# A two-layer graph attention kernel: chunk 0 and chunk 1 of the adjacency turned by column quarters, first score rows loaded from ScalarE

## The reference, cut to what matters

```
Wh = (h @ W).reshape(N, H, D)                      # layer 0: H = 4 heads, D = 32
e = leaky(s_src[:, None] + s_dst[None, :])         # 4096 x 4096 for each head
e = where(adj > 0, e, NEG_INF); attention = softmax(e, axis=1)
x = layernorm(x + elu(attention @ Wh))
...                                                # layer 1: one head over all 128 features
x = layernorm(x + proj(expmap0(attention1 @ logmap0(x))))
```

## Time and profile before

| what | value |
|---|---|
| median of 3 runs | 948.96 us (948.72 to 950.5) |
| profiled execution, its own time | 949.88 us |
| span of the profile | 946.1 us |
| TensorE busy | 840.5 us, 89% of the span |
| VectorE busy | 789.7 us, 83% |
| ScalarE busy | 660.4 us, 70% |
| GpSimd busy | 19.1 us, 2% |
| mean granted TensorE clock | 0.952 |

### The profile page before, as it was taken

One profiled execution on the slowest core, in us unless ns is written; L12 is line 12 of the kernel. 1 busy time (PEld: TensorE's weight loads), 2 busy tenths in 40 slices (PEclk: granted clock), 3 DMA queues, 4 the chain that ended last, 5 costly groups with the idle time before them and its releaser, 6 DMA issues.

```text
span 946.1 us, 23426 instructions
## 1 busy us (share of the span) xinstructions
PE 840.5 (89%) x10348; PEld 686.9 (73%) x10348; DVE 789.7 (83%) x1433; ACT 660.4 (70%) x846; POOL 19.1 (2%) x39
## 2 busy tenths in 40 slices
PE   6089699999899987999699979779999999999993
PEld 6089689988899987999699876435555555555551
DVE  4699499999988999999689998789495977777876
ACT  2598698999769998799698894876454463647112
POOL 1000000000000000000000000000000000000000
PEclk9589799999899999999799989889999999999997
DMA  8999999996577002301000505240704040321000
GB/s 151 160 184 128 193 109 140 190 125 65 113 129 97 25 2 69 69 14 14 1 14 25 124 2 112 77 101 1 208 16 90 12 89 18 84 65 37 12 18 7
DMA packets 151344, 73.06 MB, mean 77 GB/s; under 512 B 138182, under 2 KB 142792, under 8 KB 150984
## 3 DMA queue, kind: packets, MB, share of 16 engines
q1 hardware_dynamic: 146484, 54.68, 26.1%
q0 software_dynamic: 4608, 16.78, 17.2%
q10 hardware_dynamic: 148, 0.07, 0.0%
HBM read 83.96 MB, written 21.12 MB: 111 GB/s over the span
## 4 chain that ended last, share of the span: by engine, by line
PE 49%; DVE 26%; ACT 10%; SPq 5%; DMA 5%; issue 4%; POOL 0%; DVEq 0%; ACTq 0%; POOLq 0%
PE bank L552 30%; PE bank L542 19%; ACT ring L595 7%; SPq L320 5%; DVE ring L792 5%; DVE ring L805 4%; DMA adj_small<-in_adj_dram 3%; ACT below L644 3%; DVE ring L812 2%; DVE evac L819 2%; DVE ring L809 2%; DVE evac L834 1%; DMA even_masks<-adj_small 1%; DMA feat<-in_x_dram 1%; DMA s_rows<-score_rows 1%
## 5 line engine op out<-in xcount | busy, mean ns | idle before, releaser
L542 PE MATMUL bank<-moving,ring 128*128 128x99 bf16 (+1 forms) x6144 | 476.2, 224 | 27.0 <-DVE ring L812 21.3
L595 ACT ACTIVATE ring<-s_rows,scores 128x1024 fp8e4<-128x1024 f32 (+1 forms) x464 | 411.6, 975 | 71.0 <-PE bank L542 52.2
L542 PEld LDWEIGHTS bank<-moving,ring 128*128 128x128 fp8e4 x6144 | 399.0, 99 | 34.7 <-issue 18.5
L552 PE MATMUL bank<-moving,above 128*128 128x387 bf16 x1024 | 338.7, 331 | 12.3 <-DVE evac L973 6.9
L552 PE MATMUL bank<-moving,below 128*128 128x387 bf16 x1024 | 340.1, 332 | 0.0
L542 PE MATMUL bank<-moving,even_masks 128*128 128x99 bf16 x1280 | 176.1, 212 | 36.7 <-DVE ring L805 31.9
L644 ACT ACTIVATE below<-s_rows,scores 128x512 int8<-128x512 f32 x256 | 159.5, 710 | 67.1 <-PE bank L552 67.1
L552 PEld LDWEIGHTS bank<-moving,above 128*128 128x128 fp8e4 x1024 | 101.4, 99 | 84.6 <-issue 8.6
L552 PEld LDWEIGHTS bank<-moving,below 128*128 128x128 fp8e4 x1024 | 100.7, 98 | 71.8 <-issue 2.6
L542 PEld LDWEIGHTS bank<-moving,even_masks 128*128 128x128 fp8e4 x1280 | 125.5, 98 | 37.5 <-issue 26.5
L792 DVE TENSOR_SCALAR ring<-s_rows,neg_d 128x1024 uint8<-128x1024 f32 (+1 forms) x176 | 98.3, 630 | 19.1 <-DMA s_rows<-score_rows 8.8
(11 more groups left out here) (164 smaller groups left out, 527.8 us busy)
## 6 DMA issues: line engine op xcount, KB each, us to landing
adj_small<-in_adj_dram POOLq DMA_DIRECT2D x32, 512.0 KB, 14.9
s_rows<-score_rows SPq DMA_DIRECT2D x12, 512.0 KB, 5.1
s_rows<-score_rows SPq DMA_DIRECT2D x16, 256.0 KB, 3.9
feat<-in_x_dram SPq DMA_DIRECT2D x4, 512.0 KB, 5.7
values_kept<-even_masks SPq DMA_DIRECT2D x1, 2048.0 KB, 22.0
again<-adj_small SPq DMA_DIRECT2D x1, 2048.0 KB, 9.5
again<-values_kept SPq DMA_DIRECT2D x1, 2048.0 KB, 8.2
out_dram<-attended SPq DMA_DIRECT2D x7, 256.0 KB, 2.1
```

The lines of the kernel that those rows point to most:

```text
L542: last = pe.matmul(acc[:, at + lo:at + hi], mask, moving[:, h, j, lo:hi], start=first, stop=(j == T - 1), skip_group_check=True)
L552: last = pe.matmul(bank[2 * t + b][:, 0:PARTS * K1], of_tile(run[y][:, :], j, R, t * P, (t + 1) * P), moving1[:, PLACE1[j // GT], j % GT, ...
L595: last = act.activation(of_tile(below, k, rows, 0, rows), s_row(c, h), ACT.Sign, bias=scores[:, g * ju + k, h:h + 1], saturate=False)
```

## The change

Chunk 0 is cast by quarters of its columns: a quarter is 512 rows by 1024 columns, in two DMAs of 256 rows, and each of these has a first dimension of 2 (even and odd rows of `adj`), a second of 128 and 1024 contiguous elements. Each quarter is turned by two transposing DMAs of 256 rows by 1024 columns. Chunk 1 is cast as before, and turned in four quarters of four DMAs each. `clean_masks` waits only for the quarter in which its group lies. ScalarE's queue stores the scores and loads the score rows of heads 0 to 2, between the two halves of `round_head` of head 0. SP's queue loads the score rows (0, head 3) and (1, head 0) ahead of the turns of chunk 1, and stores `values_kept` and loads (1, head 1) and (1, head 2) behind them. Stages 1 and 2 of `split_head` for head 1 go behind units 0 and 1. TensorE turns x before the small matmuls with the attention vectors.

```diff
+    PARTS_IN = [4, 4, 1, 1, 1]
...
         def shrink_adj(pool, n):
-            pool.dma_start(adj_small[n * P:(n + 1) * P, :], adj_rows[n // 2, n % 2, :, :])\
-                .then_inc(small_adj_in[n % 8], 16)
+            if n < CHUNK_TILES[0]:
+                cols = slice(n * N // CHUNK_TILES[0], (n + 1) * N // CHUNK_TILES[0])
+                for u in range(CHUNK_TILES[0] // 2):
+                    pool.dma_start(adj_small[u * 2 * P:(u + 1) * 2 * P, cols].rearrange("(k p) j -> k p j", p=P),
+                                   adj_rows[u, :, :, cols]).then_inc(small_adj_in[n % 8], 16)
+            else:
+                pool.dma_start(adj_small[n * P:(n + 1) * P, :], adj_rows[n // 2, n % 2, :, :])\
+                    .then_inc(small_adj_in[n % 8], 16)
...
-            turn_adj(sp, 0, 0)
-            turn_adj(sp, 0, 1)
-            sp.wait_ge(scores_copied, 1)
-            sp.dma_start(score_rows.rearrange("k (t p) -> t k p", p=P), turned_scores).then_inc(scores_out, 16)
-            sp.wait_ge(scores_out, 16)
-            for h in range(S_SLOTS):
-                load_s(sp, 0, h)
-            sp.wait_ge(taken, T // 2)
+            for part in range(PARTS_IN[0]):
+                for k in range(CHUNK_TILES[0] * P // TURN):
+                    turn_adj(sp, 0, part, k)
+            load_s(sp, 0, 3)
+            load_s(sp, 1, 0)
+            for part in range(PARTS_IN[1]):
+                for k in range(CHUNK_TILES[1] * P // TURN):
+                    turn_adj(sp, 1, part, k)
             sp.dma_start(values_kept, values).then_inc(values_out, 16)
-            for c in range(NC - 1):
-                if c == 1:
-                    sp.wait_ge(values_out, 16)
-                    sp.wait_ge(moving_ready, H)
-                turns = CHUNK_TILES[c + 1] * P // TURN
-                for k in range(turns):
-                    turn_adj(sp, c + 1, k)
-                    if k == 0 and c > 0:
+            load_s(sp, 1, 1)
+            load_s(sp, 1, 2)
+            sp.wait_ge(values_out, 16)
+            sp.wait_ge(moving_ready, H)
+            for c in range(1, NC - 1):
+                for k in range(CHUNK_TILES[c + 1] * P // TURN):
+                    turn_adj(sp, c + 1, 0, k)
+                    if c > 1 and k == 0:
                         load_s(sp, c, 2)
-                    if k == turns // 4:
+                    if k == 1:
                         load_s(sp, c, 3)
...
+            act.wait_ge(scores_copied, 1)
+            act.dma_start(score_rows.rearrange("k (t p) -> t k p", p=P), turned_scores).then_inc(scores_out, 16)
             act.wait_ge(factors_asked, 1)
             act.activation(factors[:, :, :, :], factors[:, :, :, :], ACT.Exp).then_inc(factors_given, 1)
-            for h in range(2):
-                for q in range(2):
-                    round_head(act, h, q)
+            round_head(act, 0, 0)
+            act.wait_ge(scores_out, 16)
+            for h in range(S_SLOTS):
+                load_s(act, 0, h)
+            round_head(act, 0, 1)
...
+                if c == 0 and i in (0, 1):
+                    round_head(act, 1, i)
...
-            if g == 0:
-                wait_raw(dve, c)
+            if g % (UHS[c] // PARTS_IN[c]) == 0:
+                wait_raw(dve, c, g * PARTS_IN[c] // UHS[c])
...
-            for h in range(2):
-                for stage in range(3):
-                    split_head(dve, h, stage)
+            for stage in range(3):
+                split_head(dve, 0, stage)
+            split_head(dve, 1, 0)
...
+                if c == 0 and i in (0, 1):
+                    split_head(dve, 1, i + 1)
```

More of the change, by code:

```diff
@@ L239, in groups_cleaned, with turns_before @@
             return sum(UHS[:c])
-        def turns_before(c):
-            return sum(n * P // TURN for n in CHUNK_TILES[:c])
+        def turns_before(c, part=0):
+            return sum(CHUNK_TILES[k] * P // TURN * PARTS_IN[k] for k in range(c)) + part * CHUNK_TILES[c] * P // TURN
         def wait_unit_done(engine, u):
@@ L251, in wait_unit_done, with wait_raw @@
                 engine.wait_ge(unit_done, open_count(u + 1))
-        def wait_raw(engine, c):
-            for n in range(turns_before(c), turns_before(c + 1)):
+        def wait_raw(engine, c, part):
+            for n in range(turns_before(c, part), turns_before(c, part + 1)):
                 engine.wait_ge(raw_in[n % 4], 16 * (n // 4 + 1))
         def wait_small_adj(engine, n):
-            engine.wait_ge(small_adj_in[n % 8], 16 * (n // 8 + 1))
+            halves = CHUNK_TILES[0] // 2
+            engine.wait_ge(small_adj_in[n % 8], 16 * (n // 8 + (halves if n % 8 < CHUNK_TILES[0] else 1)))
         def wait_s(engine, c, h):
@@ L304, in fast_pool, with turn_adj, load_s @@
                 if c > 0 and n == CHUNK_AT[c]:
-                    wait_raw(pool, c - 1)
+                    for part in range(PARTS_IN[c - 1]):
+                        wait_raw(pool, c - 1, part)
                 shrink_adj(pool, n)
-        def turn_adj(sp, c, k):
-            n = turns_before(c) + k
+        def turn_adj(sp, c, part, k):
+            n = turns_before(c, part) + k
             at = CHUNK_AT[c] + k * TURN // P
-            for t in range(at, at + TURN // P):
-                wait_small_adj(sp, t)
+            if c == 0:
+                wait_small_adj(sp, part)
+            else:
+                for t in range(at, at + TURN // P):
+                    wait_small_adj(sp, t)
             if n >= 4:
                 sp.wait_ge(raw_in[n % 4], 16 * (n // 4))
-            if k == 0 and c >= 2:
+            if part == 0 and k == 0 and c >= 2:
                 sp.wait_ge(acc_ready, pairs_before(c - 1, 0))
+            wide = N // PARTS_IN[c]
+            here = slice(part * TT // PARTS_IN[c], (part + 1) * TT // PARTS_IN[c])
             dst = chunk_masks(c).bitcast(BF16).rearrange("p (t i) -> p t i", t=TT)
-            sp.dma_start_transpose(dst[:, :, k * TURN:(k + 1) * TURN],
-                                   adj_small[at * P:at * P + TURN, :].bitcast(BF16)).then_inc(raw_in[n % 4], 16)
-        def load_s(sp, c, h):
+            sp.dma_start_transpose(dst[:, here, k * TURN:(k + 1) * TURN],
+                                   adj_small[at * P:at * P + TURN, part * wide:(part + 1) * wide].bitcast(BF16))\
+                .then_inc(raw_in[n % 4], 16)
+        def load_s(engine, c, h):
             k = H * c + h
@@ L327, in load_s @@
                 before = FIRST_UNIT[c0] + (h0 + 1) * UHS[c0]
-                sp.wait_ge(signs_ready, act_count(before))
-                sp.wait_ge(compared, before - act_count(before))
-                sp.wait_ge(s_in[k % S_SLOTS], 16 * (k // S_SLOTS))
+                engine.wait_ge(signs_ready, act_count(before))
+                engine.wait_ge(compared, before - act_count(before))
+                engine.wait_ge(s_in[k % S_SLOTS], 16 * (k // S_SLOTS))
             cols = slice(CHUNK_AT[c] * P, (CHUNK_AT[c] + CHUNK_TILES[c]) * P)
-            sp.dma_start(s_row(c, h), score_rows[H + h:H + h + 1, cols].broadcast_to([P, CHUNK_TILES[c] * P]))\
+            engine.dma_start(s_row(c, h), score_rows[H + h:H + h + 1, cols].broadcast_to([P, CHUNK_TILES[c] * P]))\
                 .then_inc(s_in[k % S_SLOTS], 16)
@@ L472, in fast_pe @@
         def fast_pe(pe):
[L473 to L477, removed]
             def turn_x(n):
@@ L497, in project @@
                 last.then_inc(projected, 1)
+            pe.wait_ge(ident_ready, 1)
             turn_x(0)
+            pe.wait_ge(small_in, 48)
+            pe.wait_ge(ones_ready, 1)
+            pe.matmul(bank[4][:, 0:2 * F], ones[0:1, :], a_row, start=True, stop=True)
+            pe.matmul(bank[5][:, 0:2 * F], ones[0:1, :], a1_row, start=True, stop=True).then_inc(a_spread, 1)
+            turn_x(1)
             pe.wait_ge(proj_ready, 1)
             for n in range(T // 2):
-                if n % 2 == 0 and n // 2 + 1 < T // 4:
+                if n % 2 == 0 and 1 < n // 2 + 1 < T // 4:
                     turn_x(n // 2 + 1)
```

## The result

The changed kernel takes 962.5 us (median of 4 runs, 958.1 to 963.5) where the kernel before takes 948.8 on the same chip: 1.0131 of its time, 95% interval 1.0106 to 1.0157. It is slower, as forecast, but by 13.6 us and not by 6, and 1.5 us above the end of the range. Its profiled execution has 962.6 us, a span of 960.8 and 1.8 around it.

A forecast was written before the change was run, and what follows sets the result against it. TensorE, busy 89% of the span, was taken as the bound, so only its gaps and slow stretches could be won. Start +11.2 less 5.5 in chunk 0 gave +5.7, 955 us; range 932 to 961, the likeliest case's own 948 to 960.

The forecast's parts named there:

- Two engines a DMA, in successive pairs: Chunk 0's casts: a first dimension of 2 keeps each DMA on two engines, 20.3 us each, several at once; chance 0.56.
- Quarter 3 waits for quarter 0, so it runs from about 33 to 54 on the four idle engines: Chunk 0's last cast: starts about 33 us, once quarter 0 has landed; stretched by turns to about 57.
- Turns get 2 GB/s of each engine beside casts: Chunk 0's turns beside casts: shorter rows leave four times the former share; quarter 0's turns take about 16 us, done near 50.
- the term of +11.2: Start of TensorE's unit 0: at 61.5 us instead of 50.3, set by the masks of quarters 0 and 1.
- The bound of 65: Latest TensorE start: both DMAs of quarter 3 late and turns' requests starved as before; the other bound was 57.
- TensorE's stretch of 69.3: From TensorE's start to chunk 1's first unit: 69.3 us instead of 74.8, 5.5 less.
- The 8.6 us gap: TensorE's wait before unit 12 goes, because head 3's score row is asked for long before its use.
- 3.8 for the stages of head 1: Stages 1 and 2 of head 1 between units 0 and 2 make TensorE wait 1.2, 2.1 and 0.5 us.
- 1 to 2 at the boundary: End of chunk 0: TensorE waits a last 1 to 2 us for ScalarE, whose signs and roundings nearly fill the stage.
- Later masks covered by some 15 us: Chunk 1: its first quarter is in by 111 us, needed at about 126, so nothing waits.
- `values_kept` and TensorE's order at the start worth nothing: Moving `values_kept` behind chunk 1's turns costs nothing; the TensorE reorder, worth 0 to 0.6 us, is taken as nothing.
- Rival 1: All engines take part in each chunk 0 cast: TensorE starts at 41.8, 14 us faster, 935 us (931 to 941); chance 0.31.

The follow-up runs named there:

- experiment 4: Changed kernel with quarter 3's casts issued without the wait for quarter 0, casts still with 2 first: 962.5 us, ratio 1.013 to the kernel before.
- experiment 1: Changed kernel with chunk 0's casts naming the dimension of 128 first instead of 2 (the wide form): 929.6 us, ratio 0.978; run again, 927.7 us.

## Why the prediction was right, and where it was too small

The direction and the mechanism came out as forecast; the size did not, and the time lies outside the range, because one cast was taken to start 12 us before it did.

- *Two engines a DMA, in successive pairs.* Right: the windows have 12/16 of the wide kernel's rate with six DMAs in flight and a share 7/6 as large with seven (0.98 against 0.84), 6,966 nearly empty packets pass first, as successive pairs have it, and the reordering alone decides the sign. The Trainium skill, "DMA: Bandwidth & Descriptors", section "Why a DMA increments its semaphore by 16 and not by 1", had the count of engines as the largest number up to 16 that divides the slowest dimension of both sides, software descriptors included; casts with 2, 4 and 128 first agree. It also says that with software descriptors all 16 engines post to the semaphore: the 16 packets beyond the rows in each wide DMA are what that would look like.
- *"Quarters 0 to 2 (six DMAs, 12 engines) then start by 10.5 to 12 and land together at 31 to 34. Quarter 3 waits for quarter 0, so it runs from about 33 to 54 on the four idle engines."* **This is the step that failed**, by its starts. A narrow DMA costs GpSimd 6.49 / 6 = 1.08 us to issue (0.70 wide), and every engine also works through the nearly empty packets of the DMAs ahead: 28 GB/s in 12 to 16 us, 61 in 16 to 20. So the last rows of the six pass at 43.3, and quarter 3, issued at 35.0, starts behind them, at 45.0 and not at 33. Its own length, 24 us with its stretch (33 to 57), was right: its last row passes at 68.4. The forecast had quarter 1 turned 2.1 us behind that end (its 57 plus 2.1 gives 59.1, and not the 59.5 that it states); the turn landed 2.7 behind.
- *Turns get 2 GB/s of each engine beside casts.* Measured: 1,092 turn packets in the 12 us from 48, 68 an engine; cast rows make 0.28 MB, about 268, 67 on each of the four engines that have them. So one turn packet goes for one row, 1.5 GB/s an engine, and the twelve other engines turn no faster than the four (that experiment 4's kernel has as many with half the rows says the same). The picture was right, the measured rate a quarter below the forecast's. Quarter 0, whose turns the forecast had done near 50, is cleaned at 61.1; TensorE doesn't wait for it, as quarter 1 comes later still.
- The late start of quarter 3 puts quarter 1 at 71.2 and not 59.5, and TensorE at 73.2 and not 61.5: the term of +11.2 was +22.9. The bound of 65 for it, and with it the range, moved each DMA and each turn a little; it did not ask what a late quarter 2 does to a cast that stands behind it.
- *TensorE's stretch of 69.3.* Measured 70.1. The 8.6 us gap is gone, and TensorE waits 3.4 us after its start, where I had 3.8 for the stages of head 1 and 1 to 2 at the boundary. Right within 1.
- *Later masks covered by some 15 us.* Right in its effect: VectorE takes chunk 1's first masks at 138.95 without a wait. Their quarter had landed at 128.6, so the cover was 10 us and not 15. It rests on the quarters, not on the late start of chunk 0: experiment 1's kernel has no such wait either, and without quarters it waits 6.0 us.
- *`values_kept` and TensorE's order at the start worth nothing.* Right for the order (929.3 against 927.7); `values_kept` was not tried alone, and nobody waits for it in the trace.
- Not foreseen: the time around the span is 1.8 us and not 3.8, in the changed kernel and, at 1.8 to 2.0, in each kernel made from it, also with TensorE's old order. What it comes from was not tried.
- Rival 1 (all engines, 935) is what experiment 1 builds: 929.6 and 927.7. With 128 first its mechanism holds; the start was 45.7 and not 41.8, since the store takes 9 us among casts and not 4, and the stretch is 68.7. The rest of the difference is in the time around the span and in later stages.

The sum, with measured terms: +22.9 - 4.7 = +18.2 at the boundary, -3.5 in later stages, -2.0 around the span: +12.7 on the profiled execution, 13.6 between medians.

Open: why quarter 3's packets, issued to four engines that carry no rows, wait until those of quarters 1 and 2 are through (12,385 by 40.0 us). Being the seventh is not the reason: in the kernel without the wait the seventh DMA, issued at once behind the sixth, flows beside the six. Open too is why a wide quarter 3 still needs until about 61 us beside turns. Both rest on counts only.

## What to carry to other kernels

Before a transfer is cut into pieces, look at which dimension comes first in it on both sides: GpSimd's casts with 2 or 4 first ran on that many of the engines here, and putting the 128 first cost nothing (949.2 us against 950.1). A transfer that is late and narrow is worse than its own length, because turns that need every engine advance no faster than the engines that it holds. And that nothing waits in a trace doesn't say that a part of the change is idle: with chunk 1's quarters no engine waited for chunk 1's masks, and without them the kernel was 8.5 us slower.

## What the runs showed of the hardware that was not expected

- By its packet counts a GpSimd DMA puts the same number of packets on all 16 engines: 129 each for 256 rows on two engines (16,512 for eight), 129 for 512 rows on four (8,256 for four), 17 for 256 rows on sixteen (2,176 for eight). Each engine works through them in order (6,966 nearly empty ones before any engine is left with rows alone).
- Seven DMAs of 129 packets an engine could be outstanding; the eighth was held 18.7 us.
- GpSimd's own time for a cast of 256 rows was 1.08 us narrow and 0.70 wide.
- A cast issued at 34.3 us moved no row until 41.2, when the rows of the earlier ones were through at 40.0.
- Turns beside a narrow cast advance as slowly with two engines held as with four: 1,090 and 1,092 packets in 12 us.
